# Two-directional selective-scan kernel: convolution, projections, softplus and smaller stages moved between slots

## What is computed

```python
xn = layernorm(x)
xz = einsum('ed,bld->bel', in_proj_w, xn)            # 256 channels of x, 256 of z
def mamba_dir(xz, ...):                              # once as it is, once on reversed tokens
    u     = silu(conv4(x) + conv_bias)               # 256 x 512 a batch
    x_dbl = einsum('bdl,kd->bkl', u, xproj_w)        # 8 rows for delta, 16 for B, 16 for C
    delta = softplus(dtproj_w @ x_dbl[:8] + dt_bias)
    dA, dBx = exp(delta * A), delta * B * u          # 256 channels x 16 states x 512 tokens
    h = scan(h * dA + dBx)                           # along the tokens
    y = sum_over_states(h * C) + D * u
    return y * silu(z)
attn = out_proj_w @ (forward + backward)
q = quantize_4bit(xn @ H)                            # scale from the maximum of each token
out = x + attn + q @ ternary(ffn_w).T
```

## Time and profile before

| | us |
|---|---|
| median of 3 runs | 961.72 (961.13 to 965.54) |
| profiled execution, its own time | 959.55 |
| its span | 957.4 |
| VectorE busy | 800.7 (84%) |
| ScalarE busy | 781.2 (82%) |
| TensorE busy | 779.1 (81%) |
| GpSimd busy | 750.3 (78%) |
| mean granted clock of TensorE | 0.887 |

### The profile page before, as it was taken

The page is one execution under the profiler, slowest core; times in us unless marked ns, Lnnn a source line. Parts: engine busy times, 40 slices in busy tenths (PEclk is TensorE's granted clock), DMA queues, the critical chain, the costliest instruction groups (busy, mean ns, idle before and its releaser), DMA issues.

```text
span 957.4 us, 13831 instructions
## 1 busy us (share of the span) xinstructions
PE 779.1 (81%) x3873; PEld 386.4 (40%) x3873; DVE 800.7 (84%) x838; ACT 781.2 (82%) x1454; POOL 750.3 (78%) x454
## 2 busy tenths in 40 slices
PE   3587986979888896988879798796988789698885
PEld 1233443443534444333354444343353343444352
DVE  2278887899888878898898888788988998998994
ACT  2499995899969898699968999489995999779970
POOL 2159888788878978699887888868886898778994
PEclk9789988889887889899988999788988999898796
DMA  3434326070430606125070512506044070703400
GB/s 89 105 77 102 64 63 128 4 164 4 118 81 13 154 3 154 46 57 107 18 182 3 130 37 71 126 3 161 6 104 93 3 164 3 175 15 78 87 14 20
DMA packets 50857, 72.44 MB, mean 76 GB/s; under 512 B 6144, under 2 KB 19344, under 8 KB 50832
## 3 DMA queue, kind: packets, MB, share of 16 engines
q1 hardware_dynamic: 50400, 71.87, 32.3%
q10 hardware_dynamic: 432, 0.26, 0.1%
HBM read 60.58 MB, written 11.53 MB: 75 GB/s over the span
## 4 chain that ended last, share of the span: by engine, by line
POOL 26%; issue 22%; ACT 22%; PE 19%; DVE 8%; DMA 1%; POOLq 1%; ACTq 0%; DVEq 0%; SPq 0%
POOL hst L678 20%; ACT da L415 8%; PE pb L792 7%; ACT dbx_t L404 6%; DVE hst L569 5%; POOL dbx_t L688 3%; PE b_ps L879 3%; PE b_ps L864 3%; PE y L896 2%; POOL t_log L694 2%; PE pb L811 1%; PE pb L819 1%; PE pb L799 1%; DVE pb L523 1%; ACT xn L307 1%
## 5 line engine op out<-in xcount | busy, mean ns | idle before, releaser
L678 POOL TENSOR_TENSOR hst<-hst,c_rep 128x1024 f32<-128x1024 f32 x256 | 600.3, 2364 | 152.9 <-DVE hst L569 146.9
L569 DVE TENSOR_TENSOR_SCAN hst<-da,b_ps 128x512 f32<-128x512 f32 x512 | 584.6, 1201 | 31.5 <-PE b_ps L879 14.4
L879 PE MATMUL b_ps<-ident,dbx_t 128*128 128x128 f32 x1536 | 257.6, 308 | 129.3 <-DVE hst L569 127.7
L415 ACT ACTIVATE da<-rep,neg_a 128x511 f32<-128x511 f32 x512 | 335.1, 709 | 2.8 <-DMA rep<-d_scr 1.8
L879 PEld LDWEIGHTS b_ps<-ident,dbx_t 128*128 128x128 f32 x1536 | 187.4, 155 | 291.0 <-DVE hst L569 270.1
L404 ACT ACTIVATE dbx_t<-du_t,b_t 128x256 f32<-128x256 f32 x576 | 246.9, 495 | 2.5 <-PE b_ps L879 1.7
L896 PE MATMUL y<-hst,sum_sel 128*32 128x512 f32 x1024 | 162.6, 713 | 2.4 <-POOL hst L678 2.4
L792 PE MATMUL pb<-xnt,conv_wt 128*128 128x512 f32 x256 | 122.5, 624 | 0.8 <-ACT xnt L315 0.8
L688 POOL TENSOR_TENSOR dbx_t<-du_t,b_t 128x1024 f32<-128x1024 f32 x48 | 91.3, 1902 | 2.7 <-ACT du_t L387 2.7
L557 DVE TENSOR_TENSOR b_ps<-b_ps,b_rep 128x1024 f32<-128x1024 f32 x64 | 78.1, 1220 | 6.5 <-PE b_ps L864 6.5
L864 PE MATMUL b_ps<-t_log,spread_sel 32*128 32x512 f32 x256 | 70.2, 687 | 14.4 <-POOL t_log L740 9.0
(11 more groups left out here) (111 smaller groups left out, 581.5 us busy)
## 6 DMA issues: line engine op xcount, KB each, us to landing
rep<-d_scr SPq DMA_DIRECT2D x128, 256.0 KB, 9.2
c_rep<-bc_scr SPq DMA_DIRECT2D x64, 256.0 KB, 4.9
d_scr<-t_pos SPq DMA_DIRECT2D x15, 512.0 KB, 2.9
b_rep<-bc_scr SPq DMA_DIRECT2D x64, 64.0 KB, 2.4
x_ln<-x SPq DMA_DIRECT2D x8, 256.0 KB, 3.1
x_res<-x SPq DMA_DIRECT2D x8, 256.0 KB, 2.7
out<-x_res SPq DMA_DIRECT2D x8, 256.0 KB, 9.4
conv_wt<-conv_w SPq DMA_DIRECT2D x2, 512.0 KB, 5.9
```

The lines of the kernel that those rows point to most:

```text
L415: nc.scalar.activation(da[s % 2][:, j, 1:L], rep[d][h][:, j, 1:L], ACT.Exp, scale=neg_a[:, d, h, j, q:q + 1]).then_inc(decay_done, 1)
L569: nc.vector.tensor_tensor_scan(hst[s % RING][:, j, :], da[s % 2][:, j, :], b_ps[:, j, :], 0.0, ALU.mult, ALU.add).then_inc(scan_done, 1)
L678: nc.gpsimd.tensor_tensor(hst[s % RING][:, two, :], hst[s % RING][:, two, :], c_rep[d][:, q:q + 1, :].broadcast_to([P, 2, L]), ALU.mult).t ...
L879: ins = tr(b_ps[:, j, P * c:P * (c + 1)], dbx_t[(NX * d + q - 1) % 2][:, c, NJ * h + j, :, :].rearrange("p r e -> p (r e)"), ident[:, :])
```

## The change

The diff reorders side stages on all engines and leaves the five steps of the recurrence as they are. Nothing is computed less or more.

- **PE**: `conv` half 0 goes from slot 7 to slot 6 (d = 1: between the two halves of `inputs`; d = 0: behind them and behind `du_transposed(V, 1)`), `conv` half 1 between the halves of `inputs` in slot 7. Both `steps` stand between the halves of slot 1; `transpose_xq`, `b_transposed` and `hadamard` go to the end of slot 3 and wait for `delta_ready`; `z_proj` waits for `xqt_ready` and `bt_ready`; `du_transposed(V, 0)` of d = 1 goes to the end of slot 5, `du_transposed(V, 1)` of d = 0 to the end of slot 6.
- **ACT**: `u_sigmoid` half 0 directly behind the first `decays` of slot 0; `keep_dut(V, 1)` behind it, in slot 0 of the next unit; `inputs_t` of q = 1 chunk 1 already in slot 7; `keep_xdbl` at the end of slot 2; `softplus_in` between the halves of slot 3 and `softplus_log` behind the second `decays` of slot 3; `keep_xqt` and `keep_bt` at the end of slot 4; `guess_rstd`, `keep_longer` and `keep_xnt` move by half a slot or a slot.
- **VectorE**: `make_u` half 0 at the end of slot 7 of the unit before; `log1p` at the end of slot 2, `delta` in slot 3 between the halves; `statistics` at the end of slot 0; `token_max` at the end of slot 4; `quantize` at the end of slot 5 behind `add_residual`.
- **GpSimd**: `scales` between the halves of slot 5, `moments` at the end of slot 0, `refine` at the end of slot 3.
- **SP**: one more wait, for the sums of unit V - 2, ahead of the loads of `c_rep`.

```diff
--- before.py
+++ after.py
@@ -221,6 +221,7 @@
                 for r in range(NR):
                     sp.dma_start(b_rep[d][CB * r:CB * (r + 1), :],
                                  bc_scr[d][r:r + 1, :].broadcast_to([CB, L])).then_inc(b_loaded[d], DMA)
+                wait(sp, sum_done, SLOTS * (V - 1))
                 by_r = bc_scr[d][NS:2 * NS, :].rearrange("(q r) l -> r q l", r=NR)
                 for r in range(NR):
                     sp.dma_start(c_rep[d][CB * r:CB * (r + 1), :, :],
@@ -339,7 +340,7 @@
             def keep_bt(d, V):
                 act.wait_ge(bt_filled, V + 1)
                 wait(act, bm_pool, NX * (V - 1))
-                nc.scalar.activation(b_t[d][:, :, :], pb[:, 0, 0:NC * NS].rearrange("p (c n) -> p c n", c=NC), ACT.Copy).then_inc(bt_ready, 1)
+                nc.scalar.activation(b_t[d][:, :, :], pb[:, 1, 0:NC * NS].rearrange("p (c n) -> p c n", c=NC), ACT.Copy).then_inc(bt_ready, 1)
 
             def softplus_in(d, V):
                 wait(act, u_ready, 2 * V + 2)
@@ -430,6 +431,7 @@
             keep_dut(0, 0, 0)
             keep_dut(0, 0, 1)
             inputs_t(0, 0, 1, 0)
+            inputs_t(0, 0, 1, 1)
 
             def unit(b, d):
                 U = 2 * b + d
@@ -439,56 +441,61 @@
                 for s in range(SLOTS):
                     decays(b, d, s, 0)
                     if s == 0:
-                        if d == 0 and not first(b):
+                        if nxt:
+                            u_sigmoid(e, V, 0)
+                        if d == 1 or not first(b):
                             keep_dut(d, U, 1)
-                        inputs_t(d, U, 1, 1)
                     if s == 1:
                         inputs_t(d, U, 1, 3)
                         if nxt:
                             u_sigmoid(e, V, 1)
                     if s == 2:
+                        inputs_t(d, U, 2, 1)
+                    if s == 3:
                         if nxt:
-                            keep_xdbl(e, V)
-                        if d == 0 and not first(b):
-                            keep_xqt(b - 1)
-                        inputs_t(d, U, 2, 2)
-                        if nxt:
-                            keep_bt(e, V)
-                    if s == 3 and nxt:
-                        softplus_log(V)
+                            softplus_in(e, V)
+                        inputs_t(d, U, 2, 3)
+                    if s == 4:
                         if d == 0 and not last(b):
-                            log_var(b + 1)
-                    if s in (4, 5):
-                        inputs_t(d, U, 3, 2 * (s - 4))
+                            guess_rstd(b + 1)
+                        inputs_t(d, U, 3, 0)
+                    if s == 5:
+                        inputs_t(d, U, 3, 2)
                     if s == 6 and d == 0 and not last(b):
                         normalize(b + 1)
-                    if s == 7 and d == 0:
-                        if not last(b):
-                            keep_xnt(b + 1)
+                    if s == 7 and nxt:
                         keep_dut(e, V, 0)
+                        inputs_t(e, V, 1, 0)
                     decays(b, d, s, 1)
                     if s == 0:
                         inputs_t(d, U, 1, 2)
-                        if nxt:
-                            u_sigmoid(e, V, 0)
                     if s == 1:
                         inputs_t(d, U, 2, 0)
-                        inputs_t(d, U, 2, 1)
                     if s == 2:
-                        inputs_t(d, U, 2, 3)
+                        inputs_t(d, U, 2, 2)
                         if nxt:
-                            softplus_in(e, V)
-                    if s == 3 and d == 0 and not last(b):
-                        guess_rstd(b + 1)
-                    if s in (4, 5):
-                        inputs_t(d, U, 3, 2 * (s - 4) + 1)
-                    if s == 5 and d == 0:
-                        z_sigmoid(b)
-                    if s == 6 and d == 0:
-                        keep_longer(b)
+                            keep_xdbl(e, V)
+                    if s == 3:
+                        if nxt:
+                            softplus_log(V)
+                        if d == 0 and not last(b):
+                            log_var(b + 1)
+                    if s == 4:
+                        inputs_t(d, U, 3, 1)
+                        if d == 0 and not first(b):
+                            keep_xqt(b - 1)
+                        if nxt:
+                            keep_bt(e, V)
+                    if s == 5:
+                        if d == 0:
+                            z_sigmoid(b)
+                        inputs_t(d, U, 3, 3)
+                        if d == 0:
+                            keep_longer(b)
+                    if s == 6 and d == 0 and not last(b):
+                        keep_xnt(b + 1)
                     if s == 7 and nxt:
-                        keep_dut(e, V, 1 - d)
-                        inputs_t(e, V, 1, 0)
+                        inputs_t(e, V, 1, 1)
 
             def body(b):
                 unit(b, 0)
@@ -629,32 +636,33 @@
                 nxt = d == 0 or not last(b)
                 for s in range(SLOTS):
                     scan(b, d, s, 0)
-                    if s == 0 and nxt:
+                    if s == 0 and d == 0 and first(b):
                         make_u(e, V, 0)
                     if s == 1 and d == 0 and not first(b):
                         gate_y(b - 1, 1)
                     if s == 3 and nxt:
-                        log1p(V)
-                    if s == 5:
-                        if d == 0:
-                            gates(b, 0)
-                            gates(b, 1)
-                        else:
-                            token_max(b)
-                    if s == 6 and d == 1:
-                        quantize(b)
+                        delta(V)
+                    if s == 5 and d == 0:
+                        gates(b, 0)
+                        gates(b, 1)
                     scan(b, d, s, 1)
                     if s == 0:
                         if nxt:
                             make_u(e, V, 1)
                         if d == 0 and not first(b):
                             gate_y(b - 1, 0)
-                    if s == 1 and d == 0 and not last(b):
-                        statistics(b + 1)
-                    if s == 3 and nxt:
-                        delta(V)
-                    if s == 5 and d == 1 and not first(b):
-                        add_residual(b - 1, pb[:, 1, :])
+                        if d == 0 and not last(b):
+                            statistics(b + 1)
+                    if s == 2 and nxt:
+                        log1p(V)
+                    if s == 4 and d == 1:
+                        token_max(b)
+                    if s == 5 and d == 1:
+                        if not first(b):
+                            add_residual(b - 1, pb[:, 1, :])
+                        quantize(b)
+                    if s == 7 and not last(b):
+                        make_u(d, U + 2, 0)
 
             def body(b):
                 unit(b, 0)
@@ -749,7 +757,11 @@
                 nxt = d == 0 or not last(b)
 
                 for s in range(SLOTS):
+                    if s == 5 and d == 1:
+                        max_known(b)
                     states_times_c(b, d, s, 0)
+                    if s == 5 and d == 1:
+                        scales(b)
                     if s == 1:
                         inputs_free(U, 2)
                         inputs_t(d, 2)
@@ -761,15 +773,11 @@
                     if s == 7 and nxt:
                         inputs_free(V, 1)
                         inputs_t(e, 1)
-                    if s == 5 and d == 1:
-                        max_known(b)
                     states_times_c(b, d, s, 1)
-                    if s == 5 and d == 1:
-                        scales(b)
                     if d == 0 and not last(b):
-                        if s == 1:
+                        if s == 0:
                             moments(b + 1)
-                        if s == 4:
+                        if s == 3:
                             refine(b + 1)
 
             def body(b):
@@ -803,7 +811,7 @@
                 pe.wait_ge(xdbl_ready, V + 1)
                 wait(pe, free, count)
                 for c in range(NC):
-                    ins = mm(pb[:, 0, NS * c:NS * (c + 1)], xdbl[d][0:XC, P * c:P * (c + 1)], ident[0:XC, DR:DR + NS], start=True, stop=True)
+                    ins = mm(pb[:, 1, NS * c:NS * (c + 1)], xdbl[d][0:XC, P * c:P * (c + 1)], ident[0:XC, DR:DR + NS], start=True, stop=True)
                 ins.then_inc(bt_filled, 1)
 
             def steps(d, h, free, count):
@@ -938,45 +946,38 @@
                 for s in range(SLOTS):
                     next_inputs(s, 0)
                     if s == 1 and nxt:
-                        if d == 0 and not first(b):
```

(67 more changed lines are left out.)

## The result

The changed kernel takes 1006.48 us (median of 4 runs, 1005.62 to 1008.22) against 963.11 of the kernel before on the same chip: ratio 1.044, 95% interval 1.042 to 1.047. Its profiled execution took 1006.21 us, 46.7 more than that of before.

What follows compares the result with a forecast made beforehand. No engine has room: VectorE is first by 1 or 2 us and idles about 10 us a batch. 19 + 10 + 7 - 3 - 3 = +30 on the profiled 959.55 us gives 989.6, forecast 991; range 960 to 1012.

Steps and rivals of the forecast that it cites:

- part 2: Logarithm, 15 times: Ln ends after VectorE wants log1p; waits of 40 us against 29.4, +10 (bounds 0 to +20).
- part 1: Convolution in slots 6 and 7, 14 times: PE late, waits 46 us against 26.6, +19 (bounds +12 to +28).
- part 4: Gains: projection ends ahead of VectorE's need, -3.4; unit 0's sigmoid no longer stands behind the second decays, -3.0.
- part 3: Quantization, seven times: VectorE waits 2.7 us for the scales, 19 us against 10.7, +7 (bounds 0 to +10).
- Part 5: Remaining moves, such as SP's wait, steps and stages behind delta: at nothing; transposes' 14.4 us unchanged, bounds -10 to +10.
- Rival 1: Convolution 0 queued a slot earlier makes VectorE's waits for u and logarithm vanish: 920, or 941; chance 0.12.
- Rival 2: Waits only change places: make_u's becomes an equal one for b_ps, parts 1 and 2 near 0; 962 to 965; chance 0.08.
- Rival 3: PE's clock stays at 0.50 through slots 3, 4, 6 and 7: +30 more, 1020; chance 0.10 for over 1008.

Runs made afterwards that it cites:

- The filler: The changed kernel with two additional full matmuls on PE in slot 0 of each unit: 995.0 us, ratio 1.033.
- e2: The changed kernel with the logarithm part alone undone, on ACT and VectorE: 951.9 us, ratio 0.988 to the kernel before.
- e5: The kernel before with the logarithm part alone added, both ACT's and VectorE's halves: 1023.7 us, ratio 1.061.
- e12: The changed kernel with both the logarithm and the convolution parts undone: 941.8 us, ratio 0.978 to the kernel before.
- e3: The kernel before with the convolution part alone added: 969.4 us, ratio 1.0055.
- e1: The changed kernel with the convolution part alone undone, first sigmoid and make_u back in slot 0: 992.4 us, ratio 1.030 to the kernel before.
- e6: The kernel before with the quantization part alone added: 954.9 us, ratio 0.990.
- e10: The changed kernel with the logarithm part undone and inputs_t (q = 2, chunk 3) moved behind the logarithm: 999.4 us, ratio 1.036 to the kernel before.
- e7: The kernel before with inputs_t (q = 2, chunk 3) moved behind the logarithm: 960.1 us, ratio 0.993.

## Why the prediction was right, and where it was not

**Right: the direction and its general cause.** No room on any engine, so a stage set earlier than its inputs turns into a wait. The forecast batch of 114 to 116 us was 119.5. Two of the parts were wrong in opposite directions, and it was luck that the total came as near as it did:

| VectorE's waits, change in us over the whole run | predicted | measured |
|---|---|---|
| for Ln (part 2) | +10 | +33.4 |
| for sigmoids, copies and transposes (part 1, unit 0 in part 4) | +16 | +6.2 |
| for scales and projection (part 3, the rest of part 4) | +3.6 | +3.6 |
| all others | 0 | +2.4 |
| sum | +30 | +45.6 |

**Part 2, the logarithm, is the term that was mis-sized.** Of its 40 us of waits 62.8 came. For d = 0 the worked-out 2.3 was good (2.54, but 4.68 in unit 0); for d = 1 it gave 3.1 and 5.73 to 5.94 came. The step that failed is that ACT works without a gap from `u_sigmoid` 1 to the end of Ln. Counted from VectorE's first multiplication of unit 7 (469.36), the sigmoid of half 0 ends 0.8 earlier (0.9 worked out) and VectorE wants `log1p` at 21.5 (20.9), but Ln ends at 27.2 and not at 24.0. Between them lie the two waits of ACT, 1.24 and 1.82, 3.1 together, for `x_proj` at 1.2 GHz and for the `steps` behind it. The filler took 1.4 of that back. The stretch without a gap had been read from unit 7 of the kernel before; in eight of its 15 units ACT waits 0.29 to 1.70 us for `steps` (1.00 in unit 5).

**As the price of the logarithm's place alone,** +10 (bounds 0 to +20) was further off: 54.6 (e2 against the changed kernel) and 58 (e5). The prediction compared the wait in the whole new sequence with before's 29.4, and so could not see that the rest of the change shortens this wait (14.5 in e12) while the place lengthens it. The estimate from the two steps, 2.24 that VectorE asks earlier and 1.22 that ACT issues later in 15 units, is 52.

**Part 1, the convolution, was too high.** 46 us of waits were predicted; `make_u` at the ends of d = 0 units, the slot 7 transposes of d = 1 units and the second copies come to 34.9. By time the part cost 6 alone (e3), 10 beside the old place of the logarithm (e2 against e12) and 14 in the changed kernel (e1). The single waits came at or below the worked-out ones: `make_u` 1.98 (1.8 to 2.4), second copies mostly 0.81 to 0.85 (1.15; worked out exactly, 4.83 less 3.64 is 1.19), slot 7 of d = 1 1.29 (1.5 to 2.4), the convolution behind the idle stretch 4.30 us, 0.6 lost (0.7 to 1.5).

By the rule of the Trainium skill that the prediction weighed ("TensorE: Matmul & The Clock Gate", What's actually happening), the low clock is the default and activity releases it. The trace agrees behind the idle time: the granted clock is 0.50 from 403 to 406 us, where the convolution of unit 6 starts, and 1.00 from 406.5. But the price was looked for there only; the larger one was at `x_proj` (3.68 for 1.93), in the slot that the convolution had left.

**Part 3 and part 4.** The scales cost 7.8 in place of 10.7, where +7 was predicted, and the projection 8.7 in place of 3.4, where it was to vanish; so here too two errors balanced. They share one stretch: in unit 7 VectorE waits 1.46 for the projection, then 0.83 for the scales, 2.3 of the 2.7 given. Alone on the kernel before the part gains 10 us (e6); the bounds of 0 to +10 were for a `log1p` ahead of slot 3. In unit 0 the first `make_u` no longer waits, but the second does, 2.88 at 60.61 (0.91 before), and Ln 4.68 in place of 2.04, so what the first gave was lost again.

**Part 5** holds in the main: ACT's wait behind `delta` is 4.25 and 4.69 us (3 to 4 were given), and slot 5's exponentials are in time. Only `steps` were not free in d = 1, for the late `x_proj`.

**Rivals.** Rival 1 did not occur: the transposes of slot 7 were late by 1.29. Rival 2 is near what the convolution does alone (969.4 against its 962 to 965), not what the whole change does. Rival 3 named the right resource in the wrong slots. By the runs with parts undone, the logarithm's place was some 45 too low in the sum, the convolution some 5 too high, and what is left of the change in e12, 21.6 us below before, stood in the sum at +1 (parts 3 and 4, the stages behind `delta` at nothing).

## What to carry to other kernels

When a consumer and its producer are both moved, price the change of distance between them (here 2.24 + 1.22 us a unit) beside the new absolute wait, and ask which other part of the change pays for it. Read a stretch "without a gap" in several units before building on it. A diff of many moves can hide a gain under one bad move: here undoing the logarithm's place alone turned 1.044 into 0.988, and undoing the convolution's too gave 0.978. Where work is taken out of a slot of PE, look at the clock of what stays there.

## What the runs showed of the hardware

A busy-looking PE can be at the low level. Over 476 to 483.5 us of the changed kernel it was busy for 6.89 of 7.50 us, with no wait over 0.72, at a granted clock of 0.61. Before the clock fell at about 477.8 it had done, from 472.71 on, two sets of copies from 32 rows, a sum of states, an idle stretch of 0.72 us and part of a third set of copies. With two full matmuls added in that slot the granted clock stayed at 1.00, `x_proj` took 1.93 again, and the kernel was 11.5 us faster.

The same late chunk can cost nothing or much. In e10 PE waited 3.82 or 6.47 us in most units for the moved chunk, `x_proj` ran at 3.3 to 3.7 us, the mean clock was 0.858 against e2's 0.906, and the kernel took 47 us more. In e7 PE waited as long for it (5.3 to 6.6 us), `x_proj` kept its 1.93, and the kernel was no slower than before. The two kernels differ in the convolution's place and other stages; which of them, and how much of the 47 is the clock, was not tried apart.
